# Weighting gathered samples in thirds, and adding their four corners with one reduction

## The reference

```
offset = conv2d(x, p_w, p_b)                    # 18 numbers per pixel: dx, dy of 9 taps
m = sigmoid(conv2d(x, m_w, m_b))                # 9 masks per pixel
p = pixel + tap + offset                        # where each tap samples
lt, rb, lb, rt = the four whole pixels around p # rows and columns clipped at the edges
x_off = g_lt * x[lt] + g_rb * x[rb] + g_lb * x[lb] + g_rt * x[rt]
x_off = x_off * m
out = conv over the 9 taps of x_off with conv_w # 32 -> 32 channels
```

## Time and profile before

| | |
|---|---|
| median of 3 runs | 4143.36 us (4128.45 to 4147.88) |
| the profiled execution | 4145.0 us, its span 4143.0 us |
| busy PE, PEld, DVE | 2422.6 (58%), 1995.3 (48%), 2127.4 us (51%) |
| busy ACT, POOL | 1085.4 (26%), 2652.4 us (64%) |
| gathers, line 563 | 2592, busy 2639.0 us |
| line 844 | 288, busy 391.0 us; idle before it 689.6 us |
| mean granted TensorE clock | 0.67 |

### The profile page before, as it was taken

The page is one execution under the profiler, slowest core; times in us unless marked ns, Lnnn a source line. Parts: engine busy times, 40 slices in busy tenths (PEclk is TensorE's granted clock), DMA queues, the critical chain, the costliest instruction groups (busy, mean ns, idle before and its releaser), DMA issues.

```text
span 4143.0 us, 53002 instructions
## 1 busy us (share of the span) xinstructions
PE 2422.6 (58%) x19232; PEld 1995.3 (48%) x19232; DVE 2127.4 (51%) x4233; ACT 1085.4 (26%) x2749; POOL 2652.4 (64%) x2614
## 2 busy tenths in 40 slices
PE   4877776787777658857776478657775211111112
PEld 3656664565666646636665356446664211111112
DVE  4753225787444568855445678644447323222222
ACT  2643332443322324423223144322221100000000
POOL 1000004777777767777777777777777777777775
PEclk9976667777566677866667678756667555555555
DMA  5531003663311246633113266431113212111111
GB/s 178 176 87 31 1 1 125 185 182 102 87 50 50 89 137 181 171 80 87 51 50 104 76 191 180 108 93 50 50 49 112 73 53 62 52 51 51 52 52 49
DMA packets 192844, 373.96 MB, mean 90 GB/s; under 512 B 59312, under 2 KB 89264, under 8 KB 192576
## 3 DMA queue, kind: packets, MB, share of 16 engines
q1 hardware_dynamic: 107256, 198.54, 15.8%
q0 software_dynamic: 82944, 170.04, 15.4%
q10 hardware_dynamic: 2384, 2.00, 0.2%
HBM read 265.15 MB, written 104.33 MB: 89 GB/s over the span
## 4 chain that ended last, share of the span: by engine, by line
POOL 47%; issue 14%; PE 1%; DVE 0%; ACT 0%; POOLq 0%; DMA 0%; DVEq 0%; ACTq 0%
POOL got L563 47%; PE bank L1290 0%; PE bank L1234 0%; PE gates L1500 0%; PE bank L1295 0%; PE gates L1491 0%; PE bank L1275 0%; POOLq L560 0%; ACT kp L627 0%; DVE k L899 0%; DVE k L905 0%; DVE got L844 0%; DMA got<-sample_table,index 0%; ACT q L608 0%; DVE red L846 0%
## 5 line engine op out<-in xcount | busy, mean ns | idle before, releaser
L563 POOL DMA_INDIRECT got<-sample_table,index x2592 | 2639.0, 1018 | 1435.1 <-issue 774.4
L1416 PE MATMUL gates<-hist,whh 128*128 128x96 f32 x3040 | 638.8, 379 | 303.5 <-DVE hist L1094 302.5
L1234 PE MATMUL bank<-turned,wout 128*128 128x96 f32 x1728 | 325.2, 369 | 748.3 <-DVE x L859 507.0
L1416 PEld LDWEIGHTS gates<-hist,whh 128*128 128x128 f32 x3040 | 576.6, 283 | 374.2 <-DVE hist L1094 372.8
L844 DVE TENSOR_TENSOR got<-got,weight 128x1152 f32<-128x1152 f32 x288 | 391.0, 1358 | 689.6 <-DMA got<-sample_table,index 689.1
L1234 PEld LDWEIGHTS bank<-turned,wout 128*128 128x128 f32 x1728 | 313.6, 281 | 764.4 <-DVE turned L853 758.7
L1087 DVE TENSOR_TENSOR prod<-sig,gc 128x192 f32<-128x192 f32 x384 | 133.9, 349 | 633.3 <-ACT sig L714 633.3
L925 DVE TENSOR_REDUCE mx<-gates 128x2 f32<-128x392 f32 x576 | 295.7, 553 | 137.2 <-PE gates L1313 127.3
L1406 PE MATMUL gates<-xs,wa 128*128 128x192 bf16 x768 | 256.0, 333 | 102.5 <-ACT sig L718 65.4
L646 ACT ACTIVATE pt<-gates 98x512 f32<-98x512 f32 x384 | 217.7, 593 | 287.7 <-PE gates L1327 283.3
L1408 PE MATMUL gates<-ones,bw 96*128 96x192 bf16 x768 | 261.8, 341 | 0.0
(11 more groups left out here) (134 smaller groups left out, 3505.9 us busy)
## 6 DMA issues: line engine op xcount, KB each, us to landing
kst<-k_parts SPq DMA_DIRECT2D x96, 441.0 KB
got<-sample_table,index POOLq DMA_INDIRECT x2592
qst<-q_parts SPq DMA_DIRECT2D x96, 288.0 KB
k_parts<-kp SPq DMA_DIRECT2D x24, 882.0 KB
k_parts<-kp SPq DMA_DIRECT2D x24, 588.0 KB
q_parts<-qp SPq DMA_DIRECT2D x24, 576.0 KB
sample_table<-tab SPq DMA_DIRECT2D x8, 1568.0 KB
q_parts<-qp SPq DMA_DIRECT2D x24, 384.0 KB
```

Of the source, the lines that this page charges most:

```text
L563: pool.indirect_dma_start(out=got[:, uu % RING, n, :], out_offset=None, in_=tables[p], in_offset=bass.IndirectOffsetOnAxis(ap=at, axis=0)) ...
L1234: mm = pe.matmul(out_ps[n % 2][:, at:at + GN], wout[:, tap, :], turned[:, k % 2, tap, :], start=(tap == 0), stop=(tap == NTAP - 1))
L1416: mm = pe.matmul(gate[n][:, h:h + W], whh[:, HID * g:HID * (g + 1)], hist[:, (t - 1) % HIST, :], start=False, stop=True, skip_group_check= ...
```

## The change

`unit` multiplies in `PARTS = 3` instructions of three taps (384 floats) each, with no wait between them. One wait for the last of them follows; then one `tensor_reduce` adds the four corners of each tap and channel: it reads `got` as (tap, channel, corner), the corner innermost, whose neighbours lie 128 bytes apart, and writes `samp`. That instruction now releases the gather buffer. `red` and the semaphore `summed` are gone. The transpose and everything else stay.

```diff
+PARTS = 3
@@
-        red = sb("red", [P, NTAP, 2 * C])
@@
-        summed = sem("summed")
@@ def unit(uu):
+                taps = NTAP // PARTS
                 dve.wait_ge(gathered[slot], 16 * NTAP * (uu // RING + 1))
-                corners = got[:, slot, :, :].rearrange("p n (k c) -> p (n k) c", c=C)
-                w = weight[:, chunk, uu % CH].rearrange("p n k -> p (n k)").unsqueeze(2).to_broadcast([P, NTAP * 4, C])
-                dve.tensor_tensor(corners, corners, w, ALU.mult).then_inc(weighted, 1)
-                dve.wait_ge(weighted, uu + 1)
-                dve.tensor_tensor(red[:, :, :], got[:, slot, :, 0:2 * C], got[:, slot, :, 2 * C:4 * C], ALU.add).then_inc(reduced, 1)
+                for part in range(PARTS):
+                    of = slice(taps * part, taps * (part + 1))
+                    corners = got[:, slot, of, :].rearrange("p n (k c) -> p (n k) c", c=C)
+                    w = weight[:, chunk, uu % CH, of].rearrange("p n k -> p (n k)").unsqueeze(2).to_broadcast([P, taps * 4, C])
+                    dve.tensor_tensor(corners, corners, w, ALU.mult).then_inc(weighted, 1)
+                dve.wait_ge(weighted, PARTS * (uu + 1))
+                wait(dve, samp_turned, uu)
+                dve.tensor_reduce(samp[:, :, :], got[:, slot].rearrange("p n (k c) -> p n c k", c=C), AX.X, ALU.add).then_inc(reduced, 1)
                 dve.wait_ge(reduced, uu + 1)
-                wait(dve, samp_turned, uu)
-                dve.tensor_tensor(samp[:, :, :], red[:, :, 0:C], red[:, :, C:2 * C], ALU.add).then_inc(summed, 1)
-                dve.wait_ge(summed, uu + 1)
```

## The result

| | before | after |
|---|---|---|
| median | 4144.09 us (4128.45 to 4149.98) | 4301.47 us (4294.5 to 4303.83) |
| profiled execution, its span | 4145.0, 4143.0 us | 4303.83, 4301.9 us |
| mean granted TensorE clock | 0.67 | 0.655 |

The ratio is 1.0382 [1.0363, 1.0402]: the change makes the kernel 157 us slower.

The account below looks back on a forecast made before the run. GpSimd's gather issue was taken to bound the middle (barely) and end, VectorE's list the part before unit 72. Growth of 296 us, less 98 of waits and 25 of lead, plus 1, gave +174: 4317 us, range 4104 to 4355.

Parts of the forecast that it names:

- doubled read: In the reduction: reads 128 bytes apart take twice as long per float, 2.56 us; likeliest case, 4317 us, chance 0.50.
- The three multiplies, 1.52 us: In each unit on VectorE: three multiplies of 384 floats take 1.52 us, 0.16 us more than one.
- Do gathers get in between them?: At gaps between multiplies: left open; 20 of 27 pairs let a gather in, 0.30 us gained for a unit.
- Worth nothing, since GpSimd has to wait for buffers: On GpSimd: the 0.30 us gained per unit is lost waiting for buffers the reduction releases late, well over 200 us.
- The step of the LSTM with a unit, 5.8 us, the mean gather in the middle, 0.99: In the changed profile: such a step takes 5.8 us instead of 4.3; gathers 0.99 us instead of 1.035 if they get in.
- The reduction, 2.56 us by line 1050: In each unit: the reduction takes 2.56 us for the adds' 1.25, so the unit grows by 1.47 us.
- What a microsecond of growth costs: Up to unit 210: growth charged 0.9 times in attention, fully in LSTM and `prepare`, 296 us together.
- low bound of 0.6 for the attention: In the attention: lowest share of growth charged, from 54 us for 28 units of 3.15 us; takes 38 us off.
- Waits of VectorE that vanish, 98 us: Up to unit 210: VectorE's waits for gathers disappear as it comes late, taking 98 us off the growth.
- The lead of the ring, 25 us: At 3222 us: GpSimd up to six units ahead instead of one, saving up to 57 us at the end; 25 counted.
- Plain pace: In the reduction: strided reads cost nothing extra, 1.36 us; 4118 us, chance 0.22 with gathers let in, 0.08 with few or none.
- mild penalty: In the reduction: it takes 1.7 to 2.0 us, the unit grows 0.6 to 0.9 us; 4150 to 4210 us, chance 0.14.

Follow-up runs that it names:

- e11: Kernel before with the multiply cut into three, both adds kept, run again: 5341.27 us beside 5280.10, ratio 1.0106.
- e5: Changed kernel plus 36 VectorE instructions at its end (reductions, adds, copies at various read distances): 5426.57 us, one run, beside 5280.8 for before.
- e8: Kernel before, unchanged, traced again on another chip like the first: 4151.12 us.
- e9: Changed kernel, unchanged, traced again on another chip like the first: 4301.35 us, 1.0369 against the kernel before.
- e4: Changed kernel with the reduction adding four contiguous neighbours (wrong floats, same amount): 5359.57 us, 1.0133 against the kernel before.
- e12: Changed kernel with the table laid out so the four corners lie side by side, run again: 5374.97 us, 1.0153 against the kernel before.
- e3: Kernel before with a 995 ns dense reduction added to each unit between multiply and first add: 5232.18 us, ratio 0.9889.
- e7: Kernel before with the same dense reduction added to each unit, run again: 5226.21 us beside 5285.98, ratio 0.9888.
- e10: Kernel before with the same dense reduction added to each unit, a further run: 5245.62 us beside 5280.10, ratio 0.9924.
- e1: Kernel before with the multiply cut into three of three taps, both adds kept: 5351.23 us beside 5279.73, ratio 1.0127.
- e6: Changed kernel with the table laid out so the four corners lie side by side: 5442.67 us, one run, beside 5365.94 for before.

## Why the prediction was right, and where its steps were off

The forecast was 4317 us (4104 to 4355), by the case "doubled read"; 4301.47 came, 16 below, and slower, as the likeliest case had it. Two of its terms were wrong by much more than 16 us and in opposite directions.

- *The three multiplies, 1.52 us.* Right: 551 ns each, 1.48 us in all.
- *Do gathers get in between them?* Forecast as open, with three gaps in four. They do: of the held gathers that start under the first multiply 45 of 56 get in at the next gap, under the second 31 of 36 (76 of 92 in all, not the 76 of 84 of e11's expectation; the 11 missed under the first get in only behind the third). My 20 of 27 was short too: over the whole trace of before it is 28 of 33, and all five misses stand behind lines 905 and 910. The time of gathers beyond 0.944 us each falls from 192 to 120 us over the run, that of the gathers that start under the multiplies from 119 to 63. Of these 56 us 37 lie in the middle, 0.27 us a unit, where I had 0.30. Of the 296 gathers that start under a reduction, whose only SBUF input is `got`, none takes over 0.95 us. That fits the lock as I read it in the earlier trace rows, an instruction with two SBUF inputs keeping a gather from starting. The Trainium skill, "SBUF — State Buffer", section "Who interferes with whom", has the reduction right (it never contends). Of `tensor_tensor` it says two things: a measurement saw it stall no DMA, which is what I cited, and, with both inputs in SBUF, it contends with what GpSimd reads. By the 1.93 us of the earlier trace rows and the 1.26 us above there is a stall, so the second statement fits this case better; a gather does read its row numbers from `index` in SBUF, but no run here shows that it is this read that is held.
- *Worth nothing, since GpSimd has to wait for buffers.* Right: 278 us for the reduction, "well over 200", instead of 34.
- *The step of the LSTM with a unit, 5.8 us, the mean gather in the middle, 0.99.* 5.3 and 1.002: the first is too long by what the reduction was.
- *The reduction, 2.56 us by line 1050.* The mis-sized term: 2.12. I had taken a doubling from a kind of instruction that runs twice as fast when dense; e5's copy goes on growing from 16 to 128 bytes (1.19, 2.12 us), while reduction and two-input add go by a factor of 1.6 at once and stay there. With 158 ns taken off it is 1.70 ns per float, and of the rows I had, line 1176 (16 bytes apart, 1.83) was nearer than line 1050 (2.08 by my rule). The unit thus grew by 1.00 us, not 1.47 (2.67 and 3.67 us from its start to the transpose). With 0.9 of 86 units in the attention, as I counted, that takes 0.47 x (77 + 95 + 29) = 94 us off the sum.
- *What a microsecond of growth costs.* The mis-sized term on the other side. With the waits that vanished added back, the attention grew by 64 + 47 = 111 us for 86 units, the LSTM by 123 for 95, `prepare` by 33 for 29: 1.30, 1.30 and 1.14 us a unit, for 1.00 us of growth. I had charged 0.9, 1 and 1 times the growth. The second pair of traces (e8, e9) gives 1.17, 1.30 and 1.07, so the LSTM's price repeats and the attention's is good to some 0.1. My low bound of 0.6 for the attention, what a unit costs there on average, is far out; I take it that the units already in it had used up the room, which no run tests.
- In the LSTM part of that excess can be placed. Counted from one line 1094 to the next, the step with a unit grew from a median of 4.28 to 5.32 us, 1.04. The steps without one kept their median of 3.38, but their sums went from 248.7, 237.1 and 243.2 to 253.0, 250.0 and 249.8 us, 24 us in all. The two, 95 x 1.04 = 99 and 24, are the 123 us of the LSTM. TensorE is slower in these stages. Its groups in the LSTM of image 3, before, and then after:

```profile
L1416 PE MATMUL gates<-hist,whh 128*128 128x96 f32 x760 | 160.1, 379 | 80.3 <-DVE hist L1094 80.1
...
L1234 PE MATMUL bank<-turned,wout 128*128 128x96 f32 x198 | 37.0, 368 | 0.0
```

```profile
L1416 PE MATMUL gates<-hist,whh 128*128 128x96 f32 x760 | 167.2, 392 | 102.8 <-DVE hist L1094 102.6
...
L1234 PE MATMUL bank<-turned,wout 128*128 128x96 f32 x198 | 41.4, 399 | 0.0
```

  The mean granted clock fell there from 0.63 to 0.60, and in the attentions from 0.73, 0.74 and 0.74 to 0.71, 0.73 and 0.72. I read it so: VectorE holds TensorE up longer, a larger part of the stage runs at the lower of the two levels, 1.2 GHz, and then matmuls that have nothing to do with units take longer as well. For it speaks that the excess of the unit-less steps goes with the fall of the clock from image to image: 4, 13 and 7 us where the clock went from 0.62, 0.66 and 0.63 to 0.60; in e8 and e9 3, 13 and 8 us, with the clock from 0.62, 0.67 and 0.65 to 0.60, 0.61 and 0.61. It is argued all the same; no run holds the clock and varies the growth. For the attention's excess I have no such account.
- *Waits of VectorE that vanish, 98 us.* Right, to half a microsecond.
- *The lead of the ring, 25 us.* 15: `transform(0)` starts 174 us later and the end is 159 later. GpSimd was 1.4 units ahead at that point and not six (0.3 before).
- *The rivals.* Plain pace fell with the 2120 ns; that a dense reduction does run at it (1353 in e4, 1.36 forecast) leaves its time, 4118 us, untested, as e4 and e12 never met a chip of the first kind. The mild penalty had 1.7 to 2.0 us and up to 4210 us; the reduction missed it by 0.12 us, and its forecast, like mine, charged too little per microsecond.

The forecast with the measured sizes: 1.00 x (77 + 95 + 29) = 201, less 98 and 15, is 88 us, where 159 came. With these sizes I would have forecast some 4231 us, below the 4247 that I gave as the low end of the doubled read. The missing 71 are the stages' excess over my factors (34 in the attention, 28 in the LSTM, 4 in `prepare`) and the 5 us of scatter in image 0. So the forecast was near by luck: the price of the strided read, too high, stood in for a price per microsecond that was too low.

What is shown of the cause: the reduction's 2.12 us come from the distance of its reads (e4, e5), and in the LSTM the median step with a unit is longer by 1.04 us, where the unit grew by 1.00. That the length makes all of the 157 us is read from the stages; the runs that were to test it, e3, e7 and e10, never met a chip of the first kind.

Open: whether the length of the unit alone makes the 157 us; whether the split alone, or with the corners side by side, beats the kernel before on a chip of the first kind, as the rows might suggest (the changed kernel has 72 us less of held gathers, and e12 takes the reduction's penalty away); and what makes e3 faster and e1 slower on the others.

## What to carry to other kernels

Before merging adds into one reduction, look at the distance between the elements it reads: from 16 bytes on the instruction takes 1.6 times as long here, more than two dense adds. Another layout of the data gives the pace back (1353 ns in e6 and e12) at the price of slower writes; that the kernel gains by it is not shown. An engine with idle time in its sums has room only where a wait stands in the same stage: divide waits and units by stage, and charge a serial stage more than the growth itself, here 1.3 times in the LSTM. When a forecast comes out near, check each term on its own, as two of mine were off by 94 and 71 us and cancelled.

## What the runs showed of the hardware

- 1152 floats read by a reduction in groups of four: 1.34 to 1.35 us at a distance of up to 12 bytes, 2.07 to 2.19 from 16 bytes to 1152. An add: 1.36, 2.19 at 16 bytes, 2.13 at 128. A copy: 0.76, 1.19, 2.12. But 1.295 for line 1050, 384 bytes apart in runs of 24.
- A gather that starts under an instruction with two SBUF inputs ends 0.81 us after it, unless it gets in at the gap between two such instructions, which it did in 76 of 92 cases, though the next one stands ready. Under a reduction none was held (296).
- One and the same program takes 4147 or some 5280 us, by the chip: with equal durations of VectorE's instructions, and pauses of the engines between instructions, nearly all of them after the first gather. On the second kind changes of 1% came out in an order that the length of the unit does not give; a result belongs to the kind of chip it was taken on.
